# Splitting the first batch beside the experts, a router in two parts, keys folded before their split, and a last batch in two halves

## The reference

```
q = xn Wq;  latent = (xn Wk + xn Wv) Wdown;  k = latent Wup_k;  v = latent Wup_v     # 16 heads of 8
scores[q,k] = (q . k) / sqrt(128) * exp(-0.0001 |q - k|)      # clipped at 1e4, never reached here
attention = softmax(scores) v Wo
logits = xn Wr' + br;  the top 2 of 8 experts per token, softmax over the two logits
y_e = gelu(xn W1[e]' + b1[e]) W2[e]' + b2[e]                  # 128 -> 512 -> 128
z = sum of the two weighted y_e + xn;  experts = layernorm(z) * ln_w + ln_b
```

## Time and profile before

| | before |
|---|---|
| median of 3 timed executions | 271.71 us (271.5 to 272.08) |
| profiled execution: device time | 271.68 us |
| its span on the core | 269.4 us |
| busy in the span | PE 225.9, DVE 196.0, ACT 200.8, POOL 182.2 us |
| mean granted PE clock | 0.97 |

### The profile page before, as it was taken

The page is one execution under the profiler, slowest core; times in us unless marked ns, Lnnn a source line. Parts: engine busy times, 40 slices in busy tenths (PEclk is TensorE's granted clock), DMA queues, the critical chain, the costliest instruction groups (busy, mean ns, idle before and its releaser), DMA issues.

```text
span 269.4 us, 5034 instructions
## 1 busy us (share of the span) xinstructions
PE 225.9 (84%) x1673; PEld 122.7 (46%) x1673; DVE 196.0 (73%) x466; ACT 200.8 (75%) x335; POOL 182.2 (68%) x186
## 2 busy tenths in 40 slices
PE   0794557989999999998888888998788999999964
PEld 0572143879989899995122212222112231232313
DVE  2837986788988986874787876686967677667641
ACT  2557526445555565659999999999899999999950
POOL 9176708747787855594999999998899999700000
PEclk9998968999999999999999999999999999999995
DMA  6995601432217237311640169211890000000001
GB/s 202 438 439 202 175 22 39 133 134 79 67 53 179 68 74 188 78 27 49 184 112 23 29 164 217 61 29 33 207 202 2 1 21 20 0 39 2 1 39 45
DMA packets 17900, 27.46 MB, mean 102 GB/s; under 512 B 3008, under 2 KB 14944, under 8 KB 17488
## 3 DMA queue, kind: packets, MB, share of 16 engines
q1 hardware_dynamic: 15264, 22.21, 26.9%
q0 software_dynamic: 2272, 4.66, 7.4%
q10 hardware_dynamic: 336, 0.25, 0.4%
HBM read 13.01 MB, written 4.65 MB: 66 GB/s over the span
## 4 chain that ended last, share of the span: by engine, by line
PE 36%; ACT 29%; DVE 17%; issue 14%; DMA 2%; DVEq 2%; ACTq 0%
ACT shared L900 25%; PE ps L641 9%; PE ps L652 9%; PE ps L717 4%; PE ps L702 3%; DVE ps L1155 3%; PE ps L679 2%; PE ps L561 2%; DMA wvl<-w_router 2%; DVE shared L1016 2%; DVEq L1033 1%; PE ps L729 1%; DVE panels L1138 1%; DVE out_heads L1162 1%; PE ps L630 1%
## 5 line engine op out<-in xcount | busy, mean ns | idle before, releaser
L900 ACT ACTIVATE shared<-ps,rest_sb 128x1024 f32<-128x1024 f32 x128 | 130.1, 1153 | 1.7 <-DVE ps L1155 1.1
L1155 DVE TENSOR_TENSOR ps<-ps,mend_sb 128x256 f32<-128x256 f32 (+1 forms) x128 | 70.7, 562 | 29.8 <-PE ps L702 28.6
L869 ACT ACTIVATE shared<-ps,shared 128x128 f32<-128x128 f32 x156 | 44.5, 369 | 33.3 <-PE ps L641 33.3
L717 PE MATMUL ps<-shared,v_sb 128*9 128x512 f32 x512 | 66.9, 595 | 2.0 <-DVE out_heads L1162 1.2
L357 POOL DMA_INDIRECT shared<-xn_scr,source_i x39 | 46.5, 1192 | 29.4 <-PE ps L630 17.4
L702 PE MATMUL ps<-stacked 64*128 64x512 bf16 x256 | 49.6, 386 | 12.7 <-ACT shared L900 11.8
L702 PEld LDWEIGHTS ps<-stacked 64*128 64x128 bf16 x256 | 12.3, 92 | 81.4 <-ACT shared L900 73.7
L1036 DVE COPY shared<-panels 128x1156 f32 x39 | 38.8, 996 | 11.1 <-issue 10.8
L641 PE MATMUL ps<-shared 128*128 128x128 f32 x312 | 41.8, 277 | 2.4 <-DVE shared L1104 2.3
L652 PE MATMUL ps<-shared 128*128 128x128 f32 x312 | 41.5, 276 | 0.3 <-ACT shared L869 0.3
L641 PEld LDWEIGHTS ps<-shared 128*128 128x128 f32 x312 | 37.9, 192 | 3.6 <-DVE shared L1104 3.6
(11 more groups left out here) (156 smaller groups left out, 247.3 us busy)
## 6 DMA issues: line engine op xcount, KB each, us to landing
stacked<-parts SPq DMA_DIRECT2D x72, 128.0 KB, 2.6
panels<-weights SPq DMA_DIRECT2D x1, 4624.0 KB, 17.7
y_scr<-y_rows SPq DMA_DIRECT2D x19, 128.0 KB, 1.8
x_sb<-x_tiles SPq DMA_DIRECT2D x4, 256.0 KB, 4.7
xn_scr<-x_sb SPq DMA_DIRECT2D x1, 1024.0 KB, 9.0
xnT<-x_tiles SPq DMA_DIRECT2D x1, 1024.0 KB, 4.9
out<-panels SPq DMA_DIRECT2D x4, 256.0 KB, 2.0
shared<-xn_scr,source_i POOLq DMA_INDIRECT x39, 3.1
```

What stands on the lines that cost most here:

```text
L717: last = nc.tensor.matmul(ps[32 * g:32 * g + VW, OUT_BANK, :], v_sb[:, b * QT + tile, h, :], probs_fast[:, duo % DUO_SLOTS, g // 2, g % 2, :],
L869: last = nc.scalar.activation(hidden[:, i % 2, c, :], ps[:, i % 2, c * P:(c + 1) * P], ACT.Gelu, bias=panel[:, i % 4, 2 * F + D + c:2 * F ...
L900: nc.scalar.activation(probs_fast[:, duo % DUO_SLOTS, couple, :, :], ps[:, score_bank(n):score_bank(n) + 2, :], ACT.Exp, scale=key_fold[:, ...
L1155: nc.vector.tensor_tensor(both, both, mend_sb[:, mends].unsqueeze(1).to_broadcast([P, 2, mends.stop - mends.start]), ALU.mult).then_inc(fa ...
```

## The change

Five edits.

1. **Keys folded ahead of the split.** `key_fold` goes; the keys are multiplied by a third row of `fold` before their split, as the queries are. A split has 10 steps instead of 9, and the exponential has no per-partition scale.
2. **Router in two parts.** Tiles 0 to 5 are routed while PE still computes the others; tiles 6 to 15 after it.
3. **Batch 0's split moved.** It no longer stands ahead of the gathers; its 10 steps follow gathers 4, 6, ..., 22. `shift_again` moves to gathers 23, 25, 27 and 29. SP stacks batch 0's rows after the stores of pairs 7 (queries) and 12 (keys), where `split_left`'s rows are stacked too.
4. **PE's order among the experts.** `widen(n-1)` comes ahead of `turn_places(n)`.
5. **The last batch in two halves.** The last group's copy, turn, division, projection, sum and store are done in halves of 256 queries, each half in PSUM banks of its own.

```diff
-                     ("head_ones", NORM_ROWS), ("ranking", EXPERTS), ("key_fold", QT)):
...
-        AGAIN_AT = (14, 18, 22, 26)
+        AGAIN_AT = (23, 25, 27, 29)
+        FIRST_SPLIT_AT = 4
...
             def split_step(b, step):
+                side, at = divmod(step, 5)
+                kind, rows = ((RIGHT, qT_sb), (KEYS, kT_sb))[side]
+                into, ready = parts[:, b % 2, kind], parts_ready[kind]
...
+                    nc.gpsimd.tensor_tensor(folded[:], rows[:, b * S:(b + 1) * S], fold_sb[:, kind, :], ALU.mult).then_inc(pool_step, 1)
+                elif at == 1:
...
+                    nc.gpsimd.tensor_copy(into[:, 0, :], folded[:]).then_inc(ready, 1)
...
-            split(0)
...
                 if i in AGAIN_AT:
                     shift_again(AGAIN_AT.index(i))
+                step, odd = divmod(i - FIRST_SPLIT_AT, 2)
+                if 0 <= step < SPLIT_STEPS and not odd:
+                    split_step(0, step)
...
-            sp.wait_ge(rows_clear, 1)
-            stack_rows(0, RIGHT)
-            stack_rows(0, KEYS)
...
+                for kind, step in ((RIGHT, 5), (KEYS, SPLIT_STEPS)):
+                    if pair == (FIRST_SPLIT_AT + 2 * step) // 2:
+                        sp.wait_ge(rows_clear, 1)
+                        stack_rows(0, kind)
...
             for n in range(WORK + 1):
+                if n >= 1:
+                    widen(n - 1)
                 if n < WORK:
                     turn_places(n)
-                if n >= 1:
-                    widen(n - 1)
...
+                for half in range(2):
+                    pe.wait_ge(fast_heads, GROUPS + half)
+                    if half == 0:
+                        pe.wait_ge(fast_done, GROUPS - 1)
+                    for t in (2 * half, 2 * half + 1):
+                        last = nc.tensor.transpose(ps[:, LAST_TURN[half], t * P:(t + 1) * P], out_heads[:, t * P:(t + 1) * P], ident)
+                    last.then_inc(fast_outT, 1)
...
-                                         ACT.Exp, scale=key_fold[:, tile:tile + 1]).then_inc(fast_probs, 1)
+                                         ACT.Exp).then_inc(fast_probs, 1)
...
+            for part, tiles in enumerate((slice(0, ROUTED[0]), slice(ROUTED[0], TILES))):
+                v.wait_ge(vl_psum, part + 1)
...
+                top_one(tiles, logits[:, tiles, :], top[:, 0, tiles], first[:, tiles, :])
```

More of the change, by code:

```diff
@@ L46 @@
 STACKED = len(PRODUCTS) * 16
+SPLIT_STEPS = 10
 TOP = 2
@@ L337, in split @@
             def split(b):
-                for step in range(9):
+                for step in range(SPLIT_STEPS):
                     split_step(b, step)
-            split(0)
             batch_tiles = lambda b: slice(b * QT, (b + 1) * QT)
@@ L436, in close @@
                     if splits:
-                        split_step(2 + b, each)
+                        for n in range(each, SPLIT_STEPS):
+                            split_step(2 + b, n)
                 for n in range(each):
@@ L503, in _, with store @@
             sp.wait_ge(rows_in[LEFT][1], STACKED)
+            def store(tiles, count):
+                sp.wait_ge(out_ready, count)
+                sp.dma_start(out[:, tiles, :], z[:, tiles, :]).then_inc(stored, 16)
             with sp.If(fast == 1):
@@ L511, in _ @@
                         stack_rows(b, LEFT)
+                for b in range(B - 1):
+                    store(slice(b * QT, (b + 1) * QT), b + 1)
+                for half in range(2):
+                    store(slice(TILES - QT + 2 * half, TILES - QT + 2 * half + 2), B + half)
+                sp.wait_ge(stored, (B + 1) * 16)
             with sp.Else():
@@ L532, in _ @@
                         load_head(n + (SLOTS + u), u)
[L534 to L537 removed]
+                for b in range(B):
+                    store(slice(b * QT, (b + 1) * QT), b + 1)
+                sp.wait_ge(stored, B * 16)
         @block.tensor
@@ L847, in square_rows @@
                     nc.scalar.activation(squares[:, 2 * b + side, :], kept[:, b * S:(b + 1) * S], ACT.Square).then_inc(squares_ready, 1)
-            act.wait_ge(vl_psum, 1)
-            act.wait_ge(logits_ready, 1)
-            for bank in range(VL_BANKS):
-                keep_values(bank)
+            for part, (first, last) in enumerate(((0, 2), (2, VL_BANKS))):
+                act.wait_ge(vl_psum, part + 1)
+                act.wait_ge(logits_ready, part + 1)
+                for bank in range(first, last):
+                    keep_values(bank)
             keep_rows(0)
@@ L900, in _ @@
                     nc.scalar.activation(probs_fast[:, duo % DUO_SLOTS, couple, :, :], ps[:, score_bank(n):score_bank(n) + 2, :],
-                                         ACT.Exp, scale=key_fold[:, tile:tile + 1]).then_inc(fast_probs, 1)
+                                         ACT.Exp).then_inc(fast_probs, 1)
+                for half in range(2):
+                    tiles = slice(2 * half, 2 * half + 2)
+                    act.wait_ge(attnT_psum, B + half)
+                    nc.scalar.copy(attnT[:, TILES - QT + tiles.start:TILES - QT + tiles.stop, :],
+                                   ps[:, LAST_ATTENTION[half], :].rearrange("p (t f) -> p t f", t=QT)[:, tiles, :]).then_inc(attnT_ready, 1)
             with act.Else():
@@ L988, in _, with add_router_bias @@
-            top_one(logits[:], top[:, 0, :], first)
-            then(nc.vector.scalar_tensor_tensor(logits[:], first, -3.0e38, logits[:], ALU.mult, ALU.add))
-            top_one(logits[:], top[:, 1, :], second)
-            nc.vector.tensor_tensor(sel[:], first, second, ALU.add).then_inc(sel_ready, 1)
+            def add_router_bias(banks, count):
+                tiles = slice(banks.start * VL_TILES, (banks.stop - 1) * VL_TILES + count)
+                many = banks.stop - banks.start
+                return nc.vector.tensor_tensor(
+                    logits[:, tiles, :].rearrange("p (a k) e -> p a k e", k=count),
+                    ps[:, banks, 0:count * VL].rearrange("p a (k w) -> p a k w", w=VL)[:, :, :, D:VL],
+                    b_router[:, None, None, :].to_broadcast([P, many, count, EXPERTS]), ALU.add)
@@ new lines, in top_one @@
+            def top_one(tiles, values, largest, onehot):
+                ranks, picked = top[:, 2, tiles], pick[:, tiles, :]
+                many = tiles.stop - tiles.start
+                rank = ranking.unsqueeze(1).to_broadcast([P, many, EXPERTS])
+                wide = lambda ap: ap.unsqueeze(2).to_broadcast([P, many, EXPERTS])
+                then(nc.vector.tensor_reduce(largest, values, AX.X, ALU.max))
+                then(nc.vector.tensor_tensor(picked, values, wide(largest), ALU.is_equal))
+                then(nc.vector.tensor_tensor(picked, picked, rank, ALU.mult))
+                then(nc.vector.tensor_reduce(ranks, picked, AX.X, ALU.max))
+                then(nc.vector.tensor_tensor(onehot, rank, wide(ranks), ALU.is_equal))
@@ L1263 @@
         head_ones=np.eye(HEADS, NORM_ROWS, dtype=np.float32)[by_dim(np.repeat(np.arange(HEADS), HD)[None])[0]],
-        ranking=spread(EXPERTS - experts),
-        key_fold=np.exp(rate * place * np.where(place < S // 2, 1, -1)).reshape(QT, P).T.astype(np.float32))
+        ranking=spread(EXPERTS - experts))
     at = np.arange(S, dtype=np.float32)
```

141 lines of the change are left out of this document (75 added, 66 removed).

## The result

The changed kernel takes 281.25 us (median of 4, 280.6 to 282.66), the kernel before beside it 271.87 us (4, 271.5 to 272.08). The ratio is 1.0354, with an interval of 1.031 to 1.0397. The prediction was 268.7 us, faster; the sign is wrong. The profiled execution took 281.64 us with a span of 279.5, so 2.1 us lie around the span and the spans can be compared directly: +10.1 us.

What follows compares the result with a forecast made beforehand. It took routing as bound by a DVE-PE chain, experts by PE, attention by ACT and the tail by a chain without overlap. 271.7 - 4.0 + 5.5 - 3.0 - 1.5 = 268.7 us, range 262.5 to 275.5.

Steps and rivals of the forecast that it cites:

- Routing, -4.0 forecast: Expert choice before the gathers: router in two parts and POOL's split gone save 4.0 us (2.9 to 4.6).
- Experts, +5.5 forecast: Expert stage: POOL's moved split steps, with PE's widen ahead of the turn, cost 5.5 us (0 to +10).
- about 3.2 us after the turn: Experts: when DVE's next turned-tile copy comes after a long POOL step; the old order's widen came at 3.8 us.
- Each long instruction costs PE 0.4 to 0.7 us: Experts: PE's loss per long POOL step, 10 x 0.5 = 5 us, about 2 more for split_left.
- Two or three steps fall: Experts, turns 2 to 8: POOL steps falling where PE already waits for DVE's norms work; no separate size given.
- 0 to 1 us each of two times: Experts: DVE's wait at L1072 for a buffer, as SP's extra stacking adds 3.8 us of issue before a store.
- Rival B: Experts, turns 0 to 25: panel copies become the bound, 0.2 us a turn plus delays, +10; 275.0 us total; chance 0.24.
- Attention, -3.0 forecast: Attention: exponentials 0.093 us closer without the per-partition operand, only partly arriving: -3.0 us (-10 to 0).
- The gate at unit 75: Attention: batch 2's statistics wait for POOL's acc_ready, 2.8 us later at 202.1, so zero gain up to there.
- The wait foretold for unit 54: Attention: DVE's same wait for POOL, some 2.9 us, coming first at batch 0's statistics.
- rival C: Attention: the shorter exponential's gain arrives whole, -10 us; 261.7 us total; chance 0.08.
- Tail, -1.5 forecast: After the last outputs: halves let each step start when half the previous is done, -1.5 us (-2.2 to -0.5).

## Why the prediction was wrong, step by step

**Routing, -4.0 forecast, -4.8 measured: right**, just beyond the good end of -4.6, with PE's clock kept after 2.06 us of idleness; I had taken only a part of that.

**Experts, +5.5 forecast, +17.1 measured: the step that failed.** Its mechanism stood: panel copies behind POOL's steps, `widen` waiting for DVE's copy, more margin needed after the swap. The sizes did not, nor did the bound of +10. The step that failed is DVE's margin behind a long instruction: "about 3.2 us after the turn" for the copy of the next turned tile, against 3.8 for its `widen`, which left 0.6 us before the swap. The kernel before had this, behind the sum of the earlier trace rows:

```profile
80.84 0.27 PE L630 MATMUL ps<-chain_sb,shared 128*128 128x128 f32 x1
84.38 0.28 DVE L1104 COPY shared<-ps 128x128 f32<-128x128 f32 x1
...
84.74 1.13 PE L641 MATMUL ps<-shared 128*128 128x128 f32 x8
```

The copy ends at 84.66 and `widen` starts at 84.74, so 0.1 us was left, not 0.6. The 3.2 us fit from the end of the turn (81.11) to the start of the copy, while 3.8 is counted from about the turn's start, and the copy's own 0.28 is missing. The 0.9 us that the swap takes was sized right, and it fell on PE nearly whole: 0.82 at this sum in the kernel with the order alone. The terms, one by one:
- "Each long instruction costs PE 0.4 to 0.7 us": 10 x 0.5 was written down, with 2 more for `split_left`. The ten cost 12.4 us. Eight of them, outside the norms' turns, cost 0.60 to 1.41, 1.06 each. The swap I priced only through the steps, as a surcharge; it costs 6.1 us on the kernel before, 5.8 (276.75 - 270.98) where only the sums lie among the gathers, and 8.4 where the split lies there too. The split's move costs 1.9 us in the old order (272.86 - 270.98) and 4.5 in the new (281.25 - 276.75), each with its gain in the routing already in. Together they cost 2.6 us more than one by one.
- "Two or three steps fall" among the norms' turns 2 to 8: I named them and charged nothing extra. Two do, and PE's waits there are 1.12 and 2.87 us, since DVE's norms (three instructions of 0.68) follow the late panel. The order alone makes 0.40 and 1.50 of them; the other 2.1 us come with the steps.
- Longer matmuls had no term here and are 4.7 us, some 3.5 of them because the clock fell behind the waits of 2.87 and 2.36 us.
- "0 to 1 us each of two times" for SP's stacking. Once it was nothing and once a wait of 2.61 us with a clock of 0.55 behind it, 3.6 us up to the first exponential by the kernel with the stacking spread. I had counted the issue time (3.8 us more; 12 DMAs now take 7.7) and not that a store stands behind all of it.

Rival B had the sign and the place. It made the loss a saturation of 26 turns at 0.2 us each; the trace shows single waits of over 1 us and, between them, turns in which PE does not wait.

The page SBUF — State Buffer of the Trainium skill (section "SBUF: two separate sides"), with its exclusive lock on the shared port pair, was the reason to charge the steps to DVE at all. The traces agree for sums, subtractions and multiplications among the gathers: 2.25, 2.37 and 7.23 us for a copy of 0.76. The last of these says more than I drew from the page, for the wait goes on through instructions that POOL starts later. They don't show such a hold by a cast (last section). That a lock is the cause, and not something else that both engines use, is the page's statement; the traces show only when the copies end.

**Attention, -3.0 forecast, -0.6 measured.** The gate at unit 75 came as forecast: `acc_ready` 2.7 us later (2.8 forecast), nothing gained up to the statistics (+0.1). The wait foretold for unit 54 did not come; POOL was early enough there, and since it would only have been part of the same wait, the sum does not change by it. The sizes on both sides of the gate were wrong. Ahead of it the 76th exponential comes 72.9 us after the first, 76.8 before: DVE would have been 3.9 us early, not 7. Where nothing comes between, two exponentials are 0.904 us apart instead of 0.997, exactly the 0.093 forecast, but every eighth now comes 1.17 us behind the one before it. Behind the gate I gave PE and the clock 2 us of 4.9; they take 4.3. The clock's part was about right: from the 81st to the 89th exponential it is 10.0 us, against 9.0 before and 9.2 in the kernel with the statistics at unit 80, whose clock stayed at 1.00. PE's part was put at 0.8 and is most of the rest: in the last 31 spacings, at full clock, the gain is 1.0 us (32.4 against 33.4) where 2.9 were due, with PE busy 7.69 of 8 us and ACT 7.47. So with the statistics at unit 80 the whole attention gains 5.2 us (129.1 against 134.3), and rival C's 10 was out of reach even without POOL.

**Tail, -1.5 forecast, -1.7 measured: right in number, half of it by luck.** The last projection takes 1.16 us instead of 2.08, and that is the clock, not the halves: the kernel before ran it at a granted clock of 0.50, and four other kernels without halves (keys folded alone, router alone, and the two without sums among the gathers) took 1.16 for the same eight matmuls at a clock of 1.00. Their tails are 8.9 to 9.4 us long. Against them the halves (8.1) are worth 0.8 to 1.3 us. No kernel had the halves alone.

## What to carry to other kernels

Before an elementwise step is moved onto POOL beside a stage, ask which DVE instruction will run across it and how far DVE is ahead of PE at that point; the price is the overhang minus that lead, and an edit that takes the lead away reprices every step already there. Read that lead in the trace from the end of the copy to the start of its reader, behind the worst step and not in a quiet turn. Order edits of a stage and load edits of the same stage should be timed apart first: here the order was worth 6 us of loss by itself, and with it undone, the stacking spread and the statistics moved, the kernel was 2.2% faster than before. When an engine's work gets shorter, move the fixed places in its stream (here `STATS_AT`) with it, or the gain ends at the next gate.

## What the runs showed of the hardware

- A DVE copy that begins while POOL works can wait through a whole run of POOL instructions: 7.23 us across a gather, four sums and a multiplication, ending 0.62 us behind the last of them. POOL's next instruction was a cast, 0.06 us later, and the copy ended inside it. In the changed kernel a cast behind a gather did not hold a copy either:

```profile
71.95 0.95 POOL L351 DMA_INDIRECT shared<-xn_scr,source_i  x1 [1.74 <-PE ps L637]
72.48 1.04 DVE L1076 COPY shared<-panels 128x1156 f32 x1 [0.47 <-issue]
72.90 1.08 POOL L322 CAST parts<-folded 128x512 bf16<-128x512 f32 x1
```

- All ten such cases, in five kernels, read alike: copies of 0.98 to 1.10 us, casts of 1.08 to 1.10 in place of 0.62. That fits the small price of the four casts. It isn't a rule for all else: where the last gather is followed at once by the multiplication of the next batch's split, the copy begun in the gather took 1.01 us in the kernel before, and the multiplication 1.70 in place of 1.30. Why POOL gives way there stays open.
- PE idle for 4.68 us came back with a `widen` of 2.08 us (granted clock 0.50 from 118.7 to 122.5), idle for 2.36 us with one of 1.79, and 2.06 us in the routing left the clock at 1.00. A wait of 2.87 us among the norms' turns was followed by a `widen` of 1.26 and then a clock of 0.50 from 55 to 58. The same wait in the kernel with the stacking spread, 2.88 us, left it at 1.00 from 54 to 60. The length of one pause alone does not tell which level follows; what does stays open.
- An exponential of 1024 columns is 110 ns shorter without its per-partition operand, and where nothing comes between, two of them are 0.904 us apart instead of 0.997.
